# Expert rows sent to token order by indirect writes, and a last stage that reads plain blocks, in a two-layer transformer kernel on one core

## The reference

```python
scores = softmax(xt @ wg);  gates_k, idx_k = top_k(scores, 2);  gates_k /= sum(gates_k)
loc    = place of (choice, token) in its expert's list;  valid = loc < cap        # cap = 2048
disp[idx_k, loc] += xt * valid
out    = relu(disp @ w1 + b1) @ w2 + b2                                          # per expert
g      = silu(sum_k gates_k * valid * out[idx_k, loc])
s      = attention(xn) @ wo.T + bo
x      = x + s * g
```

## Time and profile before

| | |
|---|---|
| time, median of 3 runs | 4116.18 us (4105.35 to 4116.75) |
| profiled execution: span from first to last instruction | 4106.3 us |
| profiled execution: a time of its own | none is given; the median stands 9.9 us above the span |
| PE busy over the span | 3499.3 us (85%) |
| DVE busy | 2863.1 us (70%) |
| ACT busy | 1766.9 us (43%) |
| POOL busy | 745.4 us (18%) |
| granted TensorE clock, mean | 0.924 |
| DMA, mean | 60 GB/s |

### The profile page before, as it was taken

How to read it: one execution, slowest core, us unless ns; L and a number is a source line. 1 busy time by engine, 2 the same in 40 slices (tenths; PEclk the granted TensorE clock), 3 DMA queues, 4 the chain that set the end, 5 groups by cost and what they waited for, 6 DMA issues and landing times. The chain is left out here.

```text
span 4106.3 us, 65569 instructions
## 1 busy us (share of the span) xinstructions
PE 3499.3 (85%) x20499; PEld 1877.5 (46%) x20500; DVE 2863.1 (70%) x5100; ACT 1766.9 (43%) x2274; POOL 745.4 (18%) x968
## 2 busy tenths in 40 slices
PE   5777777777359999999999999999997999999954
PEld 2333333343113333333333333333335888888943
DVE  5777776776468777788778778787724665566556
ACT  2333333333103665666566566566673332233211
POOL 0333323233112222100000000000002121111066
PEclk9899888888658999999999999999998999999977
DMA  2121221212232221123333212223002121121077
GB/s 70 45 79 57 67 83 41 82 51 68 78 75 45 48 47 35 25 41 47 48 46 48 48 26 41 39 41 48 7 7 90 58 71 61 66 67 62 32 204 215
DMA packets 261897, 247.41 MB, mean 60 GB/s; under 512 B 92530, under 2 KB 233970, under 8 KB 261306
## 3 DMA queue, kind: packets, MB, share of 16 engines
q1 hardware_dynamic: 245178, 209.58, 21.8%
q0 software_dynamic: 16384, 33.64, 2.8%
HBM read 149.70 MB, written 92.67 MB: 59 GB/s over the span
## 5 line engine op out<-in xcount | busy, mean ns | idle before, releaser
L1313 DVE TENSOR_REDUCE at_part<-at_p 128x1 f32<-128x512 f32 (+3 forms) x2560 | 1402.1, 605 | 310.4 <-PE at_p L1197 192.2
L1294 ACT ACTIVATE at_ex<-at_st 128x1024 f32<-128x1024 f32 (+1 forms) x1280 | 1109.3, 895 | 830.8 <-PE at_st L1220 472.5
L1197 PE MATMUL at_p<-at_ks,at_qs 96*128 96x512 bf16 (+3 forms) x2560 | 838.3, 366 | 89.6 <-DVE at_part L1313 32.8
L1217 PE MATMUL at_st<-at_qs,at_ks 99*128 99x512 bf16 (+3 forms) x2560 | 713.3, 350 | 6.5 <-ACT at_ex L1294 4.9
L1234 PE MATMUL at_ob<-at_ex,at_vs 128*32 128x512 f32 (+3 forms) x5120 | 588.3, 541 | 3.6 <-ACT at_ex L1294 3.5
L1197 PEld LDWEIGHTS at_p<-at_ks,at_qs 96*128 96x128 bf16 x2560 | 248.1, 98 | 688.5 <-DVE at_part L1313 490.4
L1475 POOL DMA_INDIRECT e_xg<-s_xn,e_table x128 | 146.9, 1148 | 1978.2 <-DMA e_table<-s_table 1405.2
L1565 ACT ACTIVATE e_hh<-e_hb,e_b1now 128x512 fp32r<-128x512 f32 x256 | 176.3, 689 | 527.5 <-PE e_hb L1500 498.9
L1217 PEld LDWEIGHTS at_st<-at_qs,at_ks 99*128 99x128 bf16 x2560 | 242.0, 99 | 252.2 <-ACT at_ex L1294 97.8
L1530 PE MATMUL e_ob<-e_w2h,e_hh 128*128 128x256 f32 x1024 | 295.1, 288 | 15.5 <-DVE e_og L1623 15.5
L1532 PE MATMUL e_ob<-e_w2h,e_hl 128*128 128x256 f32 x1024 | 291.7, 285 | 0.0
(11 more groups left out here) (180 smaller groups left out, 4706.9 us busy)
## 6 DMA issues: line engine op xcount, KB each, us to landing
s_qk<-a_piece SPq DMA_DIRECT2D x192, 128.0 KB
at_qs<-s_qk SPq DMA_DIRECT2D x192, 128.0 KB
at_ks<-s_qk SPq DMA_DIRECT2D x192, 128.0 KB
s_v<-a_v SPq DMA_DIRECT2D x64, 256.0 KB, 5.5
at_vs<-s_v SPq DMA_DIRECT2D x32, 512.0 KB
e_w<-w SPq DMA_DIRECT2D x16, 1024.0 KB, 7.5
s_eo<-e_og SPq DMA_DIRECT2D x32, 512.0 KB, 2.6
a_x<-x SPq DMA_DIRECT2D x16, 512.0 KB, 5.2
```

What stands on the lines that cost most here:

```text
L1197: last = pe.matmul(out, qs[0:STACK, r, h, qt * P:(qt + 1) * P], ks[0:STACK, r, h, ch * SEG:ch * SEG + w], start=True, stop=not diag)
L1217: last = pe.matmul(out, ks[:, r, h, kt * P:(kt + 1) * P], qs[:, r, h, q0:q0 + w], start=True, stop=not diag)
L1294: ev.done(act.activation(ex[:, u % NE, 0:width], st[:, u % 2, 0:width], ACT.Exp, scale=SCALE), "ex")
L1313: ev.done(dve.tensor_reduce(part[:, at, ch:ch + 1], p1[:, n % NP1, 0:w], AX, ALU.max), "mx")
```

## The change

Where an expert's row goes is decided when it is written, not when it is read. The table now holds `choice * 8192 + token` for each slot. A slot that no token fills holds a number of its own from 16384 on (`spill`).

- `Route` loads one constant less, fills the table's start from `spill` after the loads have come, and makes `keep["mark"]` (`choice * 8192 + token`) with one small DVE instruction more.
- `attend_phase` writes `y` in token order, in pieces of 256 B at a stride of 1 KB. SP fills `eo` with zeros, 1 MB for each group, 16.8 MB in all; rows beyond an expert's capacity stay zero. SP's loop over groups is written out.
- `experts_phase`: DVE takes the token's number from the table with a bitwise and (`name_tokens`), and POOL gathers by that. POOL also sends each chunk, three chunks late, with 4 indirect writes to `eo` in token order. SP loads weights as soon as a split has freed their buffer, and a table when its rows have been sent.
- `combine_phase` has no POOL part. SP loads `y`, two blocks of `eo` and `x1` by plain DMAs, four segments ahead. The loops are written out. ACT scales the second row, and PE adds `bo` by a small bf16 matmul of three pieces. DVE mixes the rows of segment n+1 before it finishes segment n, with two buffers for `z`, `th` and the PSUM tile `sc`.

```diff
 Route.choose / find_places
-            dve.memset(zero[:], 0).then_inc(zeroed, 1)
+            dve.tensor_copy(unfilled[:], flat(spill)).then_inc(zeroed, 1)     # after the loads
-            then(dve.tensor_copy(flat(keep["slot"]), slotf[:]))
+            then(dve.tensor_scalar(destf[:], flat(spill), -float(NSLOT), None, ALU.add))
+            then(dve.tensor_copy(flat(keep["mark"]), destf[:]))
 attend_phase, SP
-                        dst = dram["y"][bass.ds(g, 1), qc * SEG:(qc + 1) * SEG, :]
+                        dst = dram["y"][b * M + qc * SEG:b * M + (qc + 1) * SEG, hg * G * HD:(hg + 1) * G * HD]
+                def fill(g):
+                    n = TOPK * T // NGROUPS
+                    dst = dram["eo"][g * n:(g + 1) * n, :].rearrange("(p r) d -> p r d", p=P)
+                    sp.dma_start(dst, empty[:].unsqueeze(1).to_broadcast([P, n // P, D])).then_inc(filled, 16)
+                for g in range(NGROUPS):
+                    if g + 2 < NGROUPS:
+                        ev.wait(sp, "pv", g, 0)
+                        load(slice(g + 2, g + 3), (g + 2) % NBUF)
+                    fill(g)
+                    group(g, g % NBUF, g + 1 < NGROUPS)
+                sp.wait_ge(filled, 16 * NGROUPS)
 experts_phase, SP
-                            ev.wait(sp, "oc", n, TT)
-                            pev.done(sp.dma_start(rows[:, q * TT:(q + 1) * TT, :], og[:, q % 2]), f"out{q % 2}")
+                    for u in range(2):
+                        xev.wait(sp, "wl", 2 * i + u, 2)
+                        load_weights(i + 1, u)
+                    for u in range(2):
+                        for k in range(2):
+                            pev.wait(sp, f"out{k}", i * (TURN // 2) + (u + 1) * NCH // 2, 0)
+                        load_table(i + 1, u)
 experts_phase, POOL
+                def send(n, u, q):
+                    ev.wait(pool, "oc", n, TT)
+                    for t in range(TT):
+                        c = q * TT + t
+                        pev.done(pool.indirect_dma_start(
+                            out=dram["eo"], out_offset=bass.IndirectOffsetOnAxis(ap=table[:, u, c:c + 1], axis=0),
+                            in_=og[:, q % 2, t, :], in_offset=None), f"out{q % 2}")
+                LATE = 3
+                def turn(i, first):
+                    for c in range(TURN):
+                        gather(i, c // NCH, c % NCH)          # waits for "named"
+                        if not first or c >= LATE:
+                            d = (c - LATE) % TURN
+                            send(i * TURN + c - LATE, d // NCH, d % NCH)
 experts_phase, DVE (between split_tokens and split_weights)
+                def name_tokens(i, u):
+                    pev.wait(dve, f"t{u}", i, 1)
+                    xev.done(dve.tensor_scalar(token[:, u], table[:, u], T - 1, None, ALU.bitwise_and), "named")
 combine_phase, SP
+                def load(n):
+                    k = n % NIN                                # NIN = 4
+                    into.done(sp.dma_start(y[:, k], of(dram["y"], n)), f"y{k}")
+                    for i in range(TOPK):
+                        into.done(sp.dma_start(rows[:, k, i], of(dram["eo"], i * NSEG + n)), f"rows{k}")
+                    into.done(sp.dma_start(x1[:, k], of(dram["x1"], n)), f"x1{k}")
+                for n in range(NSEG):
+                    ev.wait(sp, "res", n, 1)
+                    done.done(sp.dma_start(of(out_rows, n), res[:, n % 2]), f"out{n % 2}")
+                    if n + NIN < NSEG:
+                        load(n + NIN)
 combine_phase, PE
+                    for t in range(TT):
+                        into_bank = sc[:, n % 2, t // 2, (t % 2) * D:(t % 2 + 1) * D]
+                        for f in range(DC):
+                            pe.matmul(into_bank, yT[:, f, t * P:(t + 1) * P], wo[:, f, :], start=(f == 0), stop=False)
+                        last = pe.matmul(into_bank, pick[:], bias[:], start=False, stop=True)
 combine_phase, ACT
+                scale_second(0)
+                for n in range(NSEG):
+                    turned(n)                                  # two copies tb -> yT
+                    if n + 1 < NSEG:
+                        scale_second(n + 1)                    # four 128x256 copies by the gate
+                    half_tanh(n)
 combine_phase, DVE
+                mix(0)                                         # four 128x256: first row * gate + second
+                for n in range(NSEG):
+                    if n + 1 < NSEG:
+                        mix(n + 1)
+                    finish(n)                                  # three 128x1024, the last waits for x1 and out(n-2)
```

More of the change, by code:

```diff
@@ L1480, in _ @@
+                turn(0, True)
+                with pool.Fori(1, NTURN) as i:
+                    turn(i, False)
+                for c in range(TURN - LATE, TURN):
+                    send((NTURN - 1) * TURN + c, c // NCH, c % NCH)
             @block.tensor
@@ L1656, in combine_phase @@
[L1656 to L1660 removed]
+        sc = ps("sc", [P, 2, 2, SEG])
+        ev = Events(nc, ctx, "f", dict(tr=1, trc=DC, so=1, second=1, z=TT, th=1, u=1, w=1, res=1), set())
+        into = Events(nc, ctx, "fi", {f"{a}{k}": c for a, c in (("y", 1), ("x1", 1), ("rows", TOPK)) for k in range(NIN)},
+                      {f"{a}{k}" for a in ("y", "x1", "rows") for k in range(NIN)})
@@ new lines, in _, with then @@
+                for one in (ev, into, done):
+                    one.start(dve)
+                dve.sem_inc(ready, 1)
+                steps = [0]
+                def then(ins):
+                    steps[0] += 1
+                    ins.then_inc(picked, 1)
+                    dve.wait_ge(picked, steps[0])
+                then(dve.memset(pick[:], 0.0))
+                then(dve.memset(bias[:], 0.0))
+                dve.wait_ge(consts, 48)
+                for i in range(PIECE):
+                    row = slice(i * P // 4, i * P // 4 + 1)
+                    then(dve.memset(pick[row, :], 1.0))
+                    then(dve.tensor_copy(bias[row, :], bo[row, :]))
+                    if i < PIECE - 1:
+                        then(dve.tensor_copy(piece[:], bo[:]))
+                        then(dve.tensor_tensor(bo[:], bo[:], piece[:], ALU.subtract))
@@ new lines, in _, with mix @@
+                dve.sem_inc(split, 1)
+                def mix(n):
+                    k = n % NIN
+                    ev.wait(dve, "second", n, 1)
+                    if n >= 2:
+                        ev.wait(dve, "u", n - 1, 0)
+                    for t in range(TT):
+                        at = n * TT + t
+                        ev.done(dve.scalar_tensor_tensor(out=z[:, n % 2, t], in0=rows[:, k, 0, t], scalar=keep["gate"][:, 0, at:at + 1],
+                                                         in1=second[:, n % 2, t], op0=ALU.mult, op1=ALU.add), "z")
@@ L1819, in build @@
+                mix(0)
+                for n in range(NSEG):
+                    if n + 1 < NSEG:
+                        mix(n + 1)
+                    finish(n)
 def build(nc, io, out):
```

302 lines of the change are left out of this document (115 added, 187 removed).

## The result

The changed kernel takes **4046.18 us** (median of 4 executions, 4035.0 to 4052.44) against 4114.8 for the kernel before beside it (4105.35 to 4116.75): ratio 0.9835, interval 0.982 to 0.985. It was timed twice more: 0.9821 (0.9805 to 0.9837) and 0.9829 (0.9813 to 0.9846).

What follows compares the result with a forecast made beforehand. PE was taken to bound attention and experts, a latency loop the last stage, with POOL close behind. Terms -56.2 + 5.5 + 0.3 + 0.5 = -49.9 took 4116.2 to 4066 us, range 4050 to 4096.

Steps and rivals of the forecast that it cites:

- last stage: Combining stage: paced by DMA after the change, 143.0 us against 199.2, so -56.2 us.
- last tile to first constant: End of the experts stage: four exposed sends and their landing start the last stage 4 to 7 us later, taken as +5.5.
- steady experts: Experts stage between its ends: POOL's 128 added indirect writes and the earlier weight loads stay hidden, 0 us.
- DMA term: Last stage: five transfers of 0.524 MB a segment at 318 GB/s, 1.65 us each, 8.2 us a segment, set the pace.
- both old loops: Last stage before: SP's loads waiting for earlier output, 23.7 us every two segments, and POOL's gathers, 180 of 199 us; both go.
- The tail of the stage: Last stage after its last rows land: scaling 1.4, mix 1.7, two finishes of 3.9, write 3.4 behind another's 1.65 us.
- The clock: PE in the last stage: high clock after a first segment at the low one, despite idling 1.26 and about 1.7 us.
- The base: Whole kernel before: span 4106.3 us, median 9.9 above it at 4116.2, from which the -49.9 us was taken.
- PE as bound: Last stage rival: PE loses its clock between segments, 10.9 us a segment, kernel at 4112 us; chance 7%.
- a stage of latency: Last stage rival: outputs queue behind loads, 9.5 to 10.5 us a segment, +29 us, 4095; chance 18% with half-way clock case.
- an unhidden fill: Attention stage rival: the zero fill delays its groups by all it takes, +53 us, kernel at 4119; chance 3%.
- The one that ends slower: Experts stage rival: POOL's sends and DVE obstruct each other, up to 147 us, 4213, mostly 4120 to 4160; chance 4%.

Runs made afterwards that it cites:

- experiment 1: Changed kernel run again unchanged, twice: 4046.44 and 4041.73 us; the kernel before run again unchanged: 4108.89 us.
- experiment 7: Changed kernel without the writes of the first 14 output segments, so the last stage's DMA is loads alone: 4046.59 us, last stage 118.5 us.
- experiment 11: Kernel before with an unused tile of 128 bytes: 4111.91 us, ratio 0.9992; changed kernel with the token tile behind all others: 4045.23 us, 0.9828.
- experiment 6: Changed kernel with the zero fill in the attention stage doubled, 33.6 MB instead of 16.8: 4044.55 us, ratio 0.9826.

## Why the prediction missed

Term by term, profile against profile:

| | forecast | measured |
|---|---|---|
| last stage | -56.2 | -72.0 (199.2 to 127.2) |
| last tile to first constant | +5.5 | +6.7 (3.14 to 9.80) |
| Route and `empty`; `name_tokens` | +0.8 | +1.0 (+0.3, +0.7) |
| steady experts | 0 | -9.0 (781.3 to 772.3) |
| span | -49.9 | -73.3 |

This is one profile against one. The last stage comes again within 0.5 us (experiment 1); the rows of attention and steady experts scatter by more than they show.

**The step that failed is the DMA term, "318 GB/s ... 1.65 us a transfer, 8.2 us a segment".** A transfer took 1.41 us, 371 GB/s, and a segment 7.1. The mechanism (DMA-paced, PE at its high clock, both old loops gone) was right. Two things were wrong in the rate. I had divided the bytes of the earlier trace rows by the busy share, as if a full queue read 1.0. Loads fill it at 1.10 (experiment 7); if that holds for the gathers' row too, which no run shows alone, 318 x 1.10 is 350, what loads alone moved. And I took the lower row because both directions would run together. That raises the rate here: loads alone moved 349 and writes alone 348 (my 337 times the 1.03 of that queue when full), together 371. At 350 GB/s my sum gives a stage of 131 us, so the share would be 12 of the 15.8 us. At 371 it gives 125: 76 transfers x 0.24 us are 18 us, more than the miss. The rest went the other way: SP's first load went out 2.2 us after the stage began instead of 1.5, and the loads ran at 349 until the first write joined them at 3929.0. The high end of my range of rates would have put the stage at 136, still 9 too long.

**The tail of the stage** nearly held: after the last rows had landed at 4018.7, scaling 1.7, mix 1.7, two finishes of 3.7 and the write 3.4 make 14.3 us; forecast were 16, with 1.65 for a write ahead, which was already through.

**The end of the experts stage** took four sends 1.27 us apart as worked out, and 4.2 us from the last send's end to the first constant: near the upper of my bounds.

**The clock** was 0.59 in 3910:3925. Then it stayed high with idle times of 1.2 to 2.0 us, as I had taken from the earlier trace rows; behind the longest, 2.15 us, the slice read 0.74 (3951:3955). With two buffers, where PE idles up to 5.6 us, it was 0.67.

**The steady part**: some 3 us are the tiles' place (experiment 11), which no reading of the diff for its time could show; the rest is scatter: three profiles of the kernel before give 778.1 to 781.3, those of the changed one 772.3, 778.7 and 778.3. A chunk at a weight split takes 25.7 or 27.2 us, and the changed kernel had three of the long ones in its first profile and six in its second. So this row was luck, and the span's 73.3 us flatter the change; the medians differ by 69.

**The base**: I gave the profiled execution the median's 9.9 us above its span. Time less span is 1.8 to 2.4 us in every run here, so the profiled execution took some 4108.6 us, an estimate, and lay 7.6 below its median. The changed kernel's lay 11.2 below its own, so the difference stands but for some 4 us.

**The rivals.** PE as bound, a stage of latency, and an unhidden fill (experiment 6) did not come. The one that ends slower, POOL's sends in the way of the experts stage, did not show beside the first profiles, but on one chip something of its kind is there: 60 us in the steady part. I had looked for it on the port that POOL and DVE share (the Trainium skill, SBUF — State Buffer, "SBUF: two separate sides"). The traces agree with that rule only as far as a gather beside a split takes 2.4 us instead of 0.96, hidden; that the port is the reason is not shown. What costs the time on that chip lies behind the split, where PE's results are taken up late. As the kernel before loses 50 us to something alike in its last stage, the ratio stayed at 0.982 to 0.986 and the rival's sign did not follow. Why results are taken up late and SP's instructions are slow there, and whether it is the chip or that hour, is open.

## To carry to other kernels

Before dividing bytes by a busy share, find a stretch in the same trace where the queue is certainly full, with the same kind of traffic, and see what the share reads there. When a loop of latency goes, work out the rate of the resource that is next from both of its neighbours, and let the range reach to the fastest of them. An instruction that waits on an in-order queue delays what stands behind it: moving sends ahead of a gather cost 30 us with the wait for a whole chunk, and nothing with a wait for each tile.

## What the runs showed of the hardware

- Pieces of 1 KB: 349 GB/s for loads alone, 348 for writes alone, 371 with a fifth of writes mixed in (slices up to 391); 296 when half the packets are of 256 B. The busy share of the full queue reads 1.10, 1.03, 1.09 and 1.01 in these.
- An issue on SP's queue takes 0.38 to 0.51 us with room and about as long as a transfer, 1.2 to 1.9 us, without: SP itself shows that the queue is full.
- An indirect write of 128 rows of 1 KB costs POOL 0.97 us, starts 1.27 us apart, just as a gather does, with 512 B rows too.
- The same matmul of 512 columns takes 390 to 394 or 396 to 398 ns by whether a tile of 128 bytes stands ahead of its operands `xh` and `xl`.
- On one chip, while POOL issued indirect DMAs without a pause, DVE and ACT took up PE's results 3 to 28 us late, and SP took 0.70 us for instructions that take 0.03 to 0.05 elsewhere.
